# Moving a half tile of the down projection, and new orders in the prologue, in an attention and FFN kernel

## The chip, the cores and the metric

The kernel runs on one core of a Trainium2 chip. The metric is the device time of one execution in microseconds. A core has the engines PE (matmul), DVE (vector), ACT (scalar), POOL (GpSimd) and SP, which here issues all DMAs. Each engine works its own instructions in order; semaphores make it wait for the others.

## The reference, cut to what matters

```python
def reference(x, W_to_kv, W_compress, ..., W1, W2, W3):       # x: (8, 1024, 512)
    x = x + attn(layernorm(x))     # latent = x @ W_to_kv.T; c = latent @ W_compress.T; LN; q, k, v; rope;
                                   # causal softmax over 1024 positions; z = o @ W_comp2lat.T;
                                   # z @ W_to_kv + z @ W_out_res.T + b
    x = x + ffn(layernorm(x))      # W1, W3: (2048, 512), W2: (512, 2048)
    return x

def ffn(x, W1, W2, W3):
    hidden = silu(x @ W1.T) * (x @ W3.T)
    hidden = fwht(hidden)          # Walsh-Hadamard transform over 2048, normalised
    return hidden @ W2.T
```

## The kernel before

There are 8 sequences of 1024 tokens, and each is two blocks of 512 tokens (a = 0 to 15), of four tiles each. Blocks 0 and 1 (sequence 0) get their attention in a prologue. After it stands the main loop: 128 steps k = 16 s + h, one for each sequence s and each of 16 groups h of 128 hidden units. Beside the FFN of sequence s runs the attention of sequence s + 1, cut into slots; slot number and point are tied by slots(s, f), f = 7 h + i.

**A step.** The gate and the up projection of one group are made with seven products instead of eight (a Strassen-Winograd form): of W1, W3 and the tokens x there are seven forms each, in a high and a low fp16 half, and a product is six matmuls of 128x512 (L909 to L911: high by high, high by low, low by high, for two halves of the contraction). The points of a step, i = 0 to 6 in the code, are called 1 to 7 below. In the PSUM banks PF the sums are combined: copy_b (L1299, ACT) copies the first product's bank and product 3 waits for it; copy_p5 (L1305, ACT); sum_c (L1900, DVE) after product 3, for which product 5 waits; sum_e (L1904, DVE) after product 5, for which product 7 waits. silu(k, 0) (L1315, ACT) waits for product 4, silu(k, 1) for product 6. hidden(k, 1) (L1917, DVE) multiplies the second half once silu(k, 1) is there, hidden(k, 0) the first half once product 7 is there; high (L1326, ACT) and low_part (L1925, DVE) split the result into fp16 halves H in the step behind. copy_b of step k + 1 waits for hidden(k, 0), and product 2 of step k + 1 for hidden(k, 1).

**W2's product.** Each four steps fill a quarter of H; down(i) (L960 to L962) multiplies it with W2 (already transformed by Hadamard products), one half of a tile of 128 tokens at a call, six matmuls again. There are four calls in a step, behind points 2, 4, 6 and 7, from step 4 on. out_rows (L1936, DVE) adds a finished tile to the output rows; the two calls of a step stand behind sum_c and behind hidden(k, 1). Attention work of the same point stands behind down().

**The order on DVE and ACT** is written out by hand: fill(k, i) issues the attention work of point i. On DVE a step is: hidden(k - 1, 0), fill 1, low_part, fill 2, sum_c, out_rows, fill 3, (forms_low), fill 4, sum_e, (forms_low), fill 5, hidden(k, 1), out_rows, fill 6, fill 7. On ACT: copy_b, high, fill 1, copy_p5, fill 2, (forms_high), fill 3, silu(k, 0), fill 4, fill 5, silu(k, 1), fill 6, fill 7. Of attention, maxima (L1658 on) and low (L1673) on DVE and exps (L1155, with a load of the exponential's table, and L1160) on ACT lie in these fills, and rope (L1631 on). SP then transposes the probabilities by DMA (PT, L537); pv (L731, PE) waits for them, and outp (L741) for its result in halves.

**Sequence 0** has more beside it: POOL makes the forms of W1 and W3 in WF for h + 2 (L2166 on), ACT and DVE split them into WS (forms_high L1267, forms_low L1876) and SP stores them for the other sequences. W2 is scaled with a power of two that sums() (PE) and scale2() (DVE, v_s2) give, multiplied with blocks of 16 rows of a Hadamard matrix (hadamard2, L861) and split (split2, L1243 ACT, L1864 DVE).

**The prologue** ends with xtrans1 (L833 PE, L1223 ACT): the transposes of the normalised rows of blocks 0 and 1 (xnorm1, L1807 DVE). tokens_high (L1292, ACT) and tokens_low (L1882, DVE) split token parts, tokens_sum (L1892, DVE) makes the others. norms (L1195, ACT) gives the row norms of W1 and W3. Step 0 is made with eight plain block products (first_step, L920 to L922), of which one needs A21, a part of W1 split ahead (a21_high L1256, a21_low L1871). POOL can't go on with the forms of h = 0 before A21 is split. square2 (L1230, ACT) squares W2 with its output thrown into WS, slot 1.

## Time and profile before

| | |
|---|---|
| median of 3 runs | 2115.41 us (2113.53 to 2115.52) |
| the profiled execution | 2113.63 us, of which the span in the trace is 2111.8 us |
| PE busy | 2056.4 us, 97% |
| DVE, ACT, POOL busy | 1409.8 us (67%), 934.1 us (44%), 215.5 us (10%) |
| PE's granted clock, mean | 0.993 |
| products of steps, L909 | 1778 records, 381 ns each |
| W2's product, L960 | 1024 records, 379 ns each |

Matmuls are pipelined: a 128x512 one is on record with 0.38 us, and the next starts some 0.216 us behind it. Times in the trace are from the start of the span.

### The profile page before, as it was taken

To read this page: it belongs to the slowest core of one execution; us is meant where nothing else is said; L and a number is where in the kernel's file an instruction comes from. 1 tells how busy PE (TensorE), PEld (TensorE's weight loads), DVE (VectorE), ACT (ScalarE), POOL (GpSimd) and SP (SyncE) were. 2 spreads that over 40 slices of the span, in tenths; PEclk is the share of its full clock that TensorE was granted. 3 is DMA by queue.
4 is the path that set the end of the run, shared out by engine and by line. 5 is a ranking of instruction groups with operands and counts; after the bars stand their busy time and mean duration, and the time that the engine had idled before them with its cause. 6 is when DMAs were issued, how large, how long until landed. Compare 5 with 4: busy or idle time off the path is not lost. (4 is left out here: it accounts for less than half of the span.)

```text
span 2111.8 us, 26791 instructions
## 1 busy us (share of the span) xinstructions
PE 2056.4 (97%) x9838; PEld 986.4 (47%) x9838; DVE 1409.8 (67%) x2674; ACT 934.1 (44%) x1431; POOL 215.5 (10%) x196
## 2 busy tenths in 40 slices
PE   6789999999999999999999999999999999999999
PEld 3534444444444444444444444444444444444444
DVE  7887888667676676766667676766767666653333
ACT  5857454454434444353543544434444444332221
POOL 2364532101001010011001010010100100000000
PEclk9999999999999999999999999999999999999999
DMA  8544245542463324633346323643146332363211
GB/s 333 208 159 175 106 135 157 167 140 76 119 166 124 128 83 132 159 119 119 111 130 168 117 93 111 153 156 133 61 133 174 124 121 87 113 157 110 90 58 72
DMA packets 231138, 278.62 MB, mean 132 GB/s; under 512 B 178016, under 2 KB 178144, under 8 KB 225632
## 3 DMA queue, kind: packets, MB, share of 16 engines
q1 hardware_dynamic: 231008, 276.91, 42.3%
q8 instruction: 78, 1.28, 0.2%
q14 instruction: 52, 0.43, 0.1%
HBM read 194.81 MB, written 39.85 MB: 111 GB/s over the span
## 5 line engine op out<-in xcount | busy, mean ns | idle before, releaser
L909 PE MATMUL PF<-XF,WS 128*128 128x512 f16 x1778 | 676.7, 381 | 4.0 <-ACT PF L1299 2.9
L910 PE MATMUL PF<-XF,WS 128*128 128x512 f16 x1778 | 675.1, 380 | 0.0
L911 PE MATMUL PF<-XF,WS 128*128 128x512 f16 x1778 | 674.9, 380 | 0.0
L960 PE MATMUL PD<-W2S,H 128*128 128x512 f16 x1024 | 388.1, 379 | 0.0
L961 PE MATMUL PD<-W2S,H 128*128 128x512 f16 x1024 | 388.1, 379 | 0.0
L962 PE MATMUL PD<-W2S,H 128*128 128x512 f16 x1024 | 388.1, 379 | 0.0
L1315 ACT ACTIVATE SH<-PF,afs 128x512 f32<-128x512 f32 x256 | 175.0, 686 | 371.0 <-PE PF L911 369.7
L1925 DVE TENSOR_TENSOR H<-SH,H 128x1024 f16<-128x1024 f32 x128 | 165.6, 1294 | 183.2 <-ACT H L1326 182.8
L909 PEld LDWEIGHTS PF<-XF,WS 128*128 128x128 f16 x1778 | 173.9, 98 | 227.7 <-issue 33.9
L911 PEld LDWEIGHTS PF<-XF,WS 128*128 128x128 f16 x1778 | 174.2, 98 | 210.4 <-issue 1.4
L1917 DVE SCALAR_TENSOR_TENSOR SH<-PF,afs,SH 128x512 f32<-128x512 f32 x256 | 191.6, 749 | 111.8 <-ACT SH L1315 98.8
L910 PEld LDWEIGHTS PF<-XF,WS 128*128 128x128 f16 x1778 | 174.5, 98 | 185.3 <-issue 6.4
L1299 ACT ACTIVATE PF<-PF 128x512 f32<-128x512 f32 x127 | 73.9, 582 | 402.8 <-PE PF L911 284.6
L2146 POOL TENSOR_TENSOR ring<-ring,bb 128x512 f32<-128x512 f32 x56 | 81.9, 1493 | 1156.9 <-DVE V L1614 1156.9
L1936 DVE SCALAR_TENSOR_TENSOR ring<-PD,afs,ring 128x512 f32<-128x512 f32 x224 | 166.4, 743 | 15.6 <-PE PD L962 15.4
L960 PEld LDWEIGHTS PD<-W2S,H 128*128 128x128 f16 x1024 | 100.2, 98 | 120.8
L961 PEld LDWEIGHTS PD<-W2S,H 128*128 128x128 f16 x1024 | 100.2, 98 | 120.8
L962 PEld LDWEIGHTS PD<-W2S,H 128*128 128x128 f16 x1024 | 100.2, 98 | 120.8
L1904 DVE TENSOR_TENSOR PF<-PF,p 128x512 f32<-128x512 f32 x127 | 88.4, 696 | 101.2 <-PE PF L911 100.9
L1326 ACT ACTIVATE H<-SH 128x1024 f16<-128x1024 f32 x128 | 134.2, 1049 | 3.1 <-DVE SH L1917 2.8
L1900 DVE TENSOR_TENSOR PF<-PF,p 128x512 f32<-128x512 f32 x127 | 88.5, 697 | 64.0 <-PE PF L911 63.4
L1315 ACT ACT_TABLE_LOAD x57 | 73.1, 1283 | 11.2 <-DVE H L1925 10.5
(322 smaller groups left out, 2010.2 us busy)
## 6 DMA issues: line engine op xcount, KB each, us to landing
WS<-wscr SPq DMA_DIRECT2D x112, 896.0 KB, 4.9
W2S<-w2scr SPq DMA_DIRECT2D x30, 1024.0 KB, 6.5
ring<-x SPq DMA_DIRECT2D x56, 256.0 KB, 7.0
wscr<-WS SPq DMA_DIRECT2D x16, 896.0 KB, 3.8
out<-ring SPq DMA_DIRECT2D x56, 256.0 KB, 3.1
RAW<-w13t SPq DMA_DIRECT2D x16, 512.0 KB, 3.9
xraw<-xT SPq DMA_DIRECT2D x28, 256.0 KB, 5.7
XF<-w SPq DMA_DIRECT2D x13, 512.0 KB, 18.3
```

The costliest lines, as they stand in the source:

```text
L909: pe.matmul(bank, wh, th, start=i < 2 and j == 0, stop=False, skip_group_check=True)
L910: pe.matmul(bank, wh, tl, start=False, stop=False, skip_group_check=True)
L911: m = pe.matmul(bank, wl, th, start=False, stop=j == 1, skip_group_check=True)
L960: pe.matmul(PD[:, t % 2, :], th, wh, start=j == 0, stop=False)
L961: pe.matmul(PD[:, t % 2, :], th, wl, start=False, stop=False)
L962: m = pe.matmul(PD[:, t % 2, :], tl, wh, start=False, stop=j == 3)
L1315: ac.activation(SH[:, i, :], PF[:, (1 - k % 2, 2)[i], :], ACT.Silu, scale=afs[:, k % NH:k % NH + 1]).then_inc((a_sb, a_sc2)[i], 1)
L1326: ac.activation(H[:, q % 2, k % 4, 0, :], SH[:, :, :].rearrange("p i c -> p (i c)"), ACT.Copy).then_inc(a_hi, 1)
L1900: ve.tensor_tensor(PF[:, 2, :], PF[:, k % 2, :], p5[:, :], ALU.add).then_inc(v_c, 1)
L1917: ve.scalar_tensor_tensor(SH[:, i, :], PF[:, (k % 2, 3)[i], :], afs[:, 16 + h:17 + h], SH[:, i, :], ALU.mult, ALU.mult).then_inc((v_hA, v_ ...
L1925: ve.tensor_tensor(H[:, q % 2, k % 4, 1, :], SH[:, :, :].rearrange("p i c -> p (i c)"), H[:, q % 2, k % 4, 0, :], ALU.subtract).then_inc(v ...
L1936: ve.scalar_tensor_tensor(row, PD[:, t % 2, :], afs[:, 65:66], row, ALU.mult, ALU.add).then_inc(v_ev, 1)
```

## The change

DOWN_AT moves the third half tile of a step from behind product 6 to behind product 5. All else is in the prologue and in steps 0 and 1: A21's parts go to the last two forms of the low half of slot 1 of WS, so they need not wait for square2; first_step's block products come in another order, two of them ahead of xtrans1 of block 1, which now uses four banks; silu(0, 0) waits for the third instead of the second; forms_high(1) comes ahead of block 1's copies, forms_low(1) ahead of tokens_low(7); forms_high(2) goes behind silu(1, 0); the parts of the tokens come in another order; sums() uses bank U, hadamard2(0) no longer waits for v_s2, and scale2 comes one point earlier on DVE.

```diff
+DOWN_AT = (1, 3, 4, 6)
 def xf_no(s, i):
-    return 7 * s + i + 2 if s else (0, 4, 6, 1, 5, 3, 7, 2)[i] + 1
+    return 7 * s + i + 2 if s else (0, 4, 5, 1, 6, 3, 7, 2)[i] + 1
+        a21 = (WS[:, 1, 1, 5, :], WS[:, 1, 1, 6, :])
+        def xbank(a, t):
+            return (X, Y, G, U)[t] if a else (G, U)[t % 2]
...
 # PE: xtrans1
-                b, f = ((G, U), (X, Y))[a][t % 2], xs[t]
+                b, f = xbank(a, t), xs[t]
-                    w.wait_ge(a_xn, n - 2)
+                    w.wait_ge(a_xn, n - 4 if a else n - 2)
 # PE: hadamard2, sums
                 if i < 2:
-                    w.wait_ge(v_s2, 1)
-                    w.wait_ge(a_xn, 4)
+                    w.wait_ge(a_xn, 7 + i)
+                    if i == 1:
+                        w.wait_ge(v_s2, 1)
-                w.wait_ge(a_xn, 3)
-                pe.matmul(G[:, 0:2], ones.broadcast_to([128, 128]), st[:, 2:4], start=True, stop=True).then_inc(p_g2, 1)
+                w.wait_ge(a_xn, 8)
+                pe.matmul(U[:, 0:2], ones.broadcast_to([128, 128]), st[:, 2:4], start=True, stop=True).then_inc(p_g2, 1)
 # PE: first_step
-                    m = block_product((1, 1, 0, 0)[j], j, (0, 3)[j % 2], j % 2 == 0)
+                    m = block_product((1, 0)[j % 2], (0, 2, 1, 3)[j], (0, 3)[j // 2], j < 2)
...
             xtrans1(0, 3)
+            first_step(0)
+            first_step(1)
             w.wait_ge(v_x2, 8)
             xtrans1(1, 0)
...
-                    else:
+                    elif i > 1:
                         first_step(i)
-                    if i in (1, 3, 5, 6):
-                        down(4 * k + (1, 3, 5, 6).index(i) - 1)
+                    if i in DOWN_AT:
+                        down(4 * k + DOWN_AT.index(i) - 1)
 # ACT
             def a21_high():
                 w.wait_ge(g_wm, 2)
-                w.wait_ge(a_sq, 4)
-                ac.activation(WS[:, 1, 0, 6, :], WF[:, 2, :], ACT.Copy).then_inc(a_wh, 1)
+                ac.activation(a21[0], WF[:, 2, :], ACT.Copy).then_inc(a_wh, 1)
             def forms_high(h, part):
-                if h == 1 and part == 1:
-                    w.wait_ge(p_gu, gu_no(0, 4))
+                if h == 1:
+                    w.wait_ge(a_sq, 4)
...
-                w.wait_ge(p_gu, gu_no(k, ((3, 5) if k else (1, 5))[i]))
+                w.wait_ge(p_gu, gu_no(k, ((3, 5) if k else (2, 5))[i]))
             parts_o1(1, 0)
+            a21_high()
             hadamard(9)
             hadamard(10)
-            square2(3)
-            a21_high()
             norms(6, 0)
             norms(6, 1)
+            square2(3)
             forms_high(0, 0)
...
             norms(12, 1)
+            forms_high(1, 0)
+            forms_high(1, 1)
             xtrans1(1, 0)
-            norms(13, 0)
...
                 if k == 1:
-                    norms(14, 1)
+                    tokens_high(0, 4)
+                    norms(13, 1)
...
-                if split:
+                if split and k > 1:
                     forms_high(h + 1, 0)
                     forms_high(h + 1, 1)
...
                 fill(k, 3)
+                if k == 1:
+                    forms_high(2, 0)
+                    forms_high(2, 1)
 # DVE
             parts_o1(1, 0)
-            a21_low()
             norm2(0)
             inverse1(1, 1)
             norm2_root(0)
+            a21_low()
             outp1(1, 0)
+            max1(1, 2)
             forms_low(0, 0)
             forms_low(0, 1)
-            max1(1, 2)
...
             norm2(1)
+            tokens_low(0, 0)
             norm2_root(1)
...
             tokens_low(0, 3)
+            forms_low(1, 0)
             tokens_low(0, 7)
...
-                if s == 0 and f == SUMS_AT + 1:
+                if s == 0 and f == SUMS_AT:
                     scale2()
...
-                if k:
+                if k > 1:
                     hidden(k - 1, 0)
+                if k == 0:
+                    hidden(0, 0)
+                    tokens_low(0, 1)
+                    tokens_sum(0, 2)
                 if k == 1:
+                    tokens_sum(0, 4)
                     tokens_low(0, 2)
+                    tokens_low(0, 4)
                     tokens_sum(0, 6)
```

## Rows read from the trace of the kernel before

**Rows 1.** Busy time by stretch: length, then each engine's busy us, PEclk, DMA share, GB/s.
```profile
100.00:150.00 50.00, 41.07 (x153) 16.88 (x151) 42.34 (x79) 26.86 (x43) 27.94 (x22) 0.90 0.35 129
...
240.00:260.00 20.00, 19.12 (x93) 8.88 (x91) 18.44 (x35) 9.70 (x15) 17.47 (x15) 1.00 0.20 75
...
400.00:800.00 400.00, 398.62 (x1946) 192.33 (x1945) 271.75 (x528) 179.15 (x266) 23.75 (x16) 1.00 0.40 125
```

**Rows 2.** Waits of PE, whole span: us in total, times, longest.
```profile
PE XY L731 <- DMA PT<-Pl: 6.0, 7, 2.5
...
PE PF L909 <- ACT PF L1299: 2.9, 4, 0.9
```

**Rows 3.** Timelines of ACT, DVE and PE, 62 to 82: start, us, operation [idle before].
```profile
66.19 0.42 ACT L1256 ACTIVATE WS<-WX 128x256 f16<-128x256 f32 x1
...
66.63 0.43 DVE L1871 TENSOR_TENSOR WS<-WX,WS 128x256 f16<-128x256 f32 x1 [3.54 <-ACT WS L1256]
...
71.79 0.79 PE L793 MATMUL XY<-Kh,Q 128*128 128x512 f32 x1 [5.29 <-DVE ring L1795]
...
72.86 0.58 ACT L1212 ACTIVATE PT<-PF 128x512 f32<-128x512 f32 x1
...
81.49 0.71 PE L812 MATMUL PF<-PT,H 128*128 128x128 f32 x4 [1.73 <-ACT PT L1212]
```

**Rows 4.** Timelines of PE and DVE, 94 to 141.
```profile
94.08 0.94 PE L833 MATMUL XY<-cst_s,ring 128*128 128x128 f32 x4 [3.22 <-DVE ring L1807]
...
133.27 2.07 PE L861 MATMUL PD<-H,cst_s 128*128 128x512 f32 x2 [5.59 <-DVE afs L1856]
...
140.10 0.75 DVE L1864 SCALAR_TENSOR_TENSOR W2S<-PD,afs,W2S 128x512 f16<-128x512 f32 x1 [0.94 <-ACT W2S L1243]
```

**Rows 5.** Timeline of PE, two waits for transposed probabilities.
```profile
215.24 0.62 PE L731 MATMUL XY<-PT,V 128*128 128x128 f16 x8 [2.52 <-DMA PT<-Pl]
...
703.42 0.51 PE L731 MATMUL XY<-PT,V 128*128 128x128 f16 x6 [0.66 <-DMA PT<-Pl]
```

**Rows 6.** Timelines of PE and ACT, sequence 1, end of step 12.
```profile
568.48 0.38 PE L960 MATMUL PD<-W2S,H 128*128 128x512 f16 x1
...
569.77 0.38 PE L909 MATMUL PF<-XF,WS 128*128 128x512 f16 x1
...
568.68 0.69 ACT L1315 ACTIVATE SH<-PF,afs 128x512 f32<-128x512 f32 x1 [4.51 <-PE PF L911]
...
574.90 0.58 ACT L1299 ACTIVATE PF<-PF 128x512 f32<-128x512 f32 x1 [1.84 <-DVE SH L1917]
...
576.25 0.38 PE L909 MATMUL PF<-XF,WS 128*128 128x512 f16 x1
```

**Rows 7.** Sequence 2, step 13: busy time by stretch, timelines of ACT and PE.
```profile
833.41:839.08 5.67, 5.67 (x28) 2.56 (x27) 5.33 (x21) 0.91 (x1) 0.00 (x0) 1.00 0.50 169
...
839.17 0.58 ACT L1299 ACTIVATE PF<-PF 128x512 f32<-128x512 f32 x1 [4.86 <-PE PF L911]
...
840.25 0.38 PE L909 MATMUL PF<-XF,WS 128*128 128x512 f16 x1
```

**Rows 8.** The same of step 14.
```profile
847.65:853.32 5.67, 5.67 (x28) 2.59 (x27) 5.56 (x6) 0.91 (x1) 0.00 (x0) 1.00 0.47 157
...
853.41 0.58 ACT L1299 ACTIVATE PF<-PF 128x512 f32<-128x512 f32 x1 [4.85 <-PE PF L911]
...
854.50 0.38 PE L909 MATMUL PF<-XF,WS 128*128 128x512 f16 x1
```

**Rows 9.** Timelines of ACT, DVE and PE, sequence 0, steps 13 and 8.
```profile
341.63 0.58 ACT L1299 ACTIVATE PF<-PF 128x512 f32<-128x512 f32 x1 [5.43 <-DVE SH L1917]
...
342.62 0.38 PE L909 MATMUL PF<-XF,WS 128*128 128x512 f16 x1
...
250.98 0.75 DVE L1917 SCALAR_TENSOR_TENSOR SH<-PF,afs,SH 128x512 f32<-128x512 f32 x1
...
258.77 0.39 PE L909 MATMUL PF<-XF,WS 128*128 128x512 f16 x1 [0.88 <-ACT PF L1299]
```

More of the change, by code:

```diff
@@ L119, in xf_no, with t_no @@
 def xf_no(s, i):
-    return 7 * s + i + 2 if s else (0, 4, 6, 1, 5, 3, 7, 2)[i] + 1
+    return 7 * s + i + 2 if s else (0, 4, 5, 1, 6, 3, 7, 2)[i] + 1
+def t_no(s, i):
+    return 4 * s + ({1: 1, 4: 2, 2: 3, 6: 4} if s else {1: 1, 2: 2, 4: 3, 6: 4})[i]
 def wform_no(h, part):
@@ L917, in block_product @@
                 for j in range(2):
-                    wh, wl = (WS[:, f == 2, m, (0, 1, 6, 3)[f], j * 128:(j + 1) * 128] for m in range(2))
+                    wh, wl = (b[:, j * 128:(j + 1) * 128] for b in (a21 if f == 2 else (WS[:, 0, m, f, :] for m in range(2))))
                     th, tl = (XF[:, m, XPART[i], :].rearrange("p (t f c) -> p f t c", t=4, f=2)[:, j] for m in range(2))
@@ L1222, in xtrans1 @@
                 w.wait_ge(p_cp, 8)
-                ac.activation(XS[:, a, :, t * 128:(t + 1) * 128], ((G, U), (X, Y))[a][t % 2].rearrange("p (j c) -> p j c", j=4),
+                ac.activation(XS[:, a, :, t * 128:(t + 1) * 128], xbank(a, t).rearrange("p (j c) -> p j c", j=4),
                               ACT.Copy).then_inc(a_xn, 1)
@@ L1277, in tokens_high @@
                 else:
-                    w.wait_ge(v_t, 4 * s + {1: 1, 4: 2, 2: 3, 6: 4}[i])
+                    w.wait_ge(v_t, t_no(s, i))
                 if s == 0:
@@ L1419, in _ @@
             norms(9, 0)
+            norms(9, 1)
             exps1(1, 3)
@@ L1428, in _ @@
             trans1(1, 3, 1)
-            norms(9, 1)
+            norms(10, 0)
             parts_o1(1, 2)
-            norms(10, 0)
+            norms(10, 1)
             parts_o1(1, 3)
-            norms(10, 1)
             xtrans1(0, 0)
-            norms(11, 0)
             xtrans1(0, 1)
-            norms(11, 1)
             xtrans1(0, 2)
@@ L1441, in _ @@
             tokens_high(0, 3)
+            norms(11, 0)
+            norms(11, 1)
             norms(12, 0)
             norms(12, 1)
+            forms_high(1, 0)
+            forms_high(1, 1)
             xtrans1(1, 0)
-            norms(13, 0)
             xtrans1(1, 1)
-            norms(13, 1)
             xtrans1(1, 2)
@@ L1494, in _ @@
                 if k == 1:
-                    norms(15, 0)
+                    norms(14, 0)
                 fill(k, 0)
@@ L1499, in _ @@
                 if k == 1:
+                    norms(14, 1)
+                    tokens_high(0, 6)
+                    norms(15, 0)
                     norms(15, 1)
-                    tokens_high(0, 6)
                 fill(k, 1)
-                if split:
+                if split and k > 1:
                     forms_high(h + 1, 0)
@@ L1508, in _ @@
                     silu(k, 0)
-                else:
-                    tokens_high(0, 4)
                 fill(k, 3)
+                if k == 1:
+                    forms_high(2, 0)
+                    forms_high(2, 1)
                 fill(k, 4)
@@ L1515, in _ @@
                 if k == 0:
-                    norms(14, 0)
+                    norms(13, 0)
                     tokens_high(0, 2)
@@ L1846, in scale2 @@
                 w.wait_ge(p_g2, 1)
-                k = sv.mark(ve.tensor_copy(st[:, 4:6], G[:, 0:2]))
+                k = sv.mark(ve.tensor_copy(st[:, 4:6], U[:, 0:2]))
                 sv.after(k)
@@ L1870, in a21_low @@
                 w.wait_ge(a_wh, 1)
-                ve.tensor_tensor(WS[:, 1, 1, 6, :], WF[:, 2, :], WS[:, 1, 0, 6, :], ALU.subtract).then_inc(v_wl, 1)
+                ve.tensor_tensor(a21[1], WF[:, 2, :], a21[0], ALU.subtract).then_inc(v_wl, 1)
             def forms_low(h, part):
                 w.wait_ge(a_wh, wform_no(h, part))
+                if h == 1 and part == 1:
+                    w.wait_ge(p_gu, gu_no(0, 4))
                 f = slice(0, 4) if part == 0 else slice(4, 7)
@@ L1886, in tokens_sum @@
                 w.wait_ge(v_xs if s else a_xn, tile_no(2 * s + 1, 3))
-                w.wait_ge(v_t, 4 * s + {1: 0, 4: 1, 2: 2, 6: 3}[i])
+                w.wait_ge(v_t, t_no(s, i) - 1)
                 w.wait_ge(v_xf, xf_no(s, {1: 0, 4: 0 if s else 7, 2: 1, 6: 3}[i]))
@@ L2044, in _ @@
             xnorm1(1, 1)
-            tokens_low(0, 0)
             xnorm1(1, 2)
@@ L2051, in _ @@
             tokens_sum(0, 1)
-            tokens_sum(0, 4)
-            tokens_low(0, 1)
-            forms_low(1, 0)
             forms_low(1, 1)
-            tokens_sum(0, 2)
-            tokens_low(0, 4)
             def fill(k, j):
```

## The prediction

> **What bounds the kernel now.** I read the stages first [rows 1], then who PE waited for in all [rows 2], then the timelines around the long waits [rows 3 to 5]. From 400 to 800 us PE is busy 398.62 of 400 us, and the stages after it look the same: an edit there can win tenths of a microsecond at a place, but it can lose as much as it likes, because nothing is left to absorb a new wait. The start is different: 41.07 of 50 us between 100 and 150. The longest waits are 5.3 us for a DVE eviction [rows 3], 3.2 us for a normalised row and 5.6 us for the scale of W2 [rows 4], and 6.0 us in seven waits for transposed probabilities [rows 2]. So the edits at the start are worth something, up to the point where DVE or ACT is the next late one, and the edit of the steady step must be judged by cover, not by work. PE's work is the same in both kernels; only idle time can change.
>
> **The unit.** A product of a step, or a half tile of W2's product, is six matmuls. The half tile that starts at 568.48 is followed by product 7 at 569.77: 1.29 us [rows 6]. I write the seven products as 1 to 7 and a half tile as H. Before: 1 2 H 3 4 H 5 6 H 7 H. After: 1 2 H 3 4 H 5 H 6 7 H. Product 7 ends when it did, product 6 ends 1.29 us later, and attention work in the fifth place comes 1.29 us later.
>
> **Part 1, the moved half tile: what it covers.** In the fifth place PE waits for a DMA transpose: 2.52 us at 215.24, and 0.66 us at 703.42 [rows 5]; the latter stands for six of one kind, one for each of the sequences 1 to 6, 6.0 - 2.5 = 3.5 us together [rows 2]. H now stands ahead of it. The transposes don't depend on product 6, so the six go (-3.5 us) and the first shrinks by 1.3 us.
>
> **Part 1, what it uncovers.** Product 6 releases ACT's second silu, which releases DVE's second hidden(), behind which stand the eviction of a tile, attention's or the next tokens' DVE work and then the first hidden(). That releases ACT's copy_b, and product 3 of the next step waits for copy_b. Product 3 does not move. So wherever this chain runs without a gap, its cover shrinks by 1.29 us.
> - Step 12 (h = 12) of sequences 1 to 6: silu 568.68, the exponential's table load right behind it, then the high and low halves of the probabilities, hidden(), copy_b at 574.90 for 0.58 us. It ends at 575.48, its semaphore takes 0.06 us, and product 3 starts at 576.25 [rows 6]: cover 0.71 us, new wait 1.29 - 0.71 = 0.58 us.
> - Step 13: DVE is busy 5.33 of the 5.67 us between the second hidden() and the end of the first. What is missing is small gaps between nine dependent 128x4 operations, which can't take up a delay. copy_b 839.17 + 0.58 + 0.06 against product 3 at 840.25: cover 0.44, new wait 0.85 us [rows 7].
> - Step 14: DVE 5.56 of 5.67 us; copy_b 853.41 ends 853.99, product 3 at 854.50: cover 0.45, new wait 0.84 us [rows 8].
> Each wait delays the following products too, and by the next second hidden() DVE is again waiting for PE, so they add up: 2.27 us a sequence, 13.6 us in six. The last sequence has no attention beside it and DVE has room.
> - Sequence 0, where forms are split as well: in step 13 copy_b at 341.63 ends 342.21, product 3 starts at 342.62, cover 0.35: +0.9 us. In step 8 the wait for copy_b is there already, 0.88 us at 258.77, and the second hidden() at 250.98 comes 1.1 us after product 6; it would come at about 252.1: +1.1 us [rows 9]. Before step 4 there is no half tile.
> - The other steps are at no cost: either silu is late for another reason (table load or keys on ACT), or the DVE chain has real gaps (over 2 us in step 4), or the cover is 1.3 us or more. With that cover gone each would cost up to 1.3 us. The second half tile itself needs the low half of H, which is there over 3.5 us before, so its earlier place costs nothing; the eviction of a tile does not wait for it in either kernel, so it gains nothing.
> Sum of part 1: -3.5 - 1.3 + 13.6 + 0.9 + 1.1 = **+10.8 us**.
>
> **Part 2, the start.** *A21's parts:* the low part stood ahead of the root and eviction on DVE and waited 3.54 us for ACT, where the high part at 66.19 stood behind a square of W2 [rows 3]. Now ACT makes it near 63.2, DVE does the roots first and the eviction ends near 67.1, so the scores at 71.79 start some 4.6 us earlier. Next late is ACT, busy throughout: GpSimd's forms come 0.7 us earlier, and the copy at 72.86, for which PE's next transposes wait, starts near 72.2. The square and two norms that were moved leave exps1(1,3) 1.4 us earlier. Behind it the products with P, at 81.49, start 1.3 us earlier, and all up to B11's transposes with them.
> *Two products ahead of B1's transposes:* they fill the 3.22 us wait that ends at 94.08 [rows 4], but they need B11's low part, on DVE behind the second norm: near 91.8. The forms of h = 1 (1.8 us on ACT) now stand ahead of the four copies of B1's transposes, so scale_rows, which waits for the last copy, holds the third product to about 98.7. By this sum step 1 starts 1.7 us earlier. SP is passed by nothing here; its stores and loads of forms follow the same releases.
> *The scale of W2:* sums() uses another bank, the first product with 16-row blocks no longer waits for the scale, and scale2 comes ahead of two bn_stats (1.5 us) on DVE. Against it, forms_high(2) moved behind the latent copy, and forms_low(2), ahead of sums() on DVE, waits for it till near 120.8; the tokens' last parts too are later. The scale comes at about 132.0, and the 5.59 us wait at 133.27 becomes one near 2.3 us before the second such product. PE would be 4 to 5 us ahead there, but then DVE is late: its second split of W2 at 140.10 [rows 4] moves to about 137.9, 2.2 us earlier, and DVE has hardly a gap from there to 160. I take **-2.2 us**. Bounds: all three long waits gone (5.29 + 3.22 + 5.59) would be -14.1 and can't hold with DVE and ACT full; a start in which the new orders lose on ACT what they win on PE is +0.5. For the range I take -5 to +0.5.
>
> **A rule weighed.** Behind the wait at 258.77 [rows 9] the matmuls keep their pitch: the granted clock between 240 and 260 us is 1.00, the 2.4 GHz level [rows 1]. The Trainium skill, *TensorE: Matmul & The Clock Gate*, section *A second HAM failure mode: psum-queue depth-cycling*, says that short idle times of PE between groups of matmuls can make the clock oscillate; by that rule each new wait would be dearer (rival D). The trace speaks against it.
> The page *ScalarE: Activation LUTs*, section *What ACT_TABLE_LOAD costs* in the Trainium skill, adds a drain of about 1.38 us to a switch. Here the exponential follows its 1.28 us load at once. With the drain step 12 would have had no cover at all and a new wait of 1.29 us; the sum would be 4 us higher.
>
> **The sum.** +10.8 - 2.2 = +8.6 us on a span of 2111.8 us and a run of 2113.6 us: 2122.2 us. The median of the runs shown is 1.8 us above the profiled one, so the forecast is **2124 us**, +0.4%.
>
> **Rivals.**
> - A, faster: the chain behind product 6 has more give than I read, in that DVE and ACT catch up before copy_b. The place is steps 12 to 14, the price of each 0.6 to 0.85 us; it decides once less than 0.4 us of the 1.29 us reaches copy_b. Then only the gains stand: -3.5 - 1.3 - 2.2 = -7 us, 2108. For it: out-of-phase gaps exist in other steps. Against: the two windows of DVE, 94 and 98% busy [rows 7, 8]. Chance 0.12.
> - B, no change: the start wins 6 to 8 us, since one of the shifts above isn't eaten by the next engine (the 5.6 us wait and the 1.2 GHz behind it), and part 1 costs what I say: about +4 us, 2119. Chance 0.15.
> - C, the change does less than it says: the half tile covers nothing, as another wait (the copy of ol to the output product, 0.1 us of cover left) takes the place of the six: +3.5 more, 2127.5. Chance 0.05.
> - D, the clock: PE drops to 1.2 GHz at each of some 20 new waits, as it did at the 5.59 us one, behind which the matmul pair took 2.07 us [rows 4]. A product of 1.29 us at half the clock costs 1.3 us more: +26 us, 2150. Against it, the short waits of before left the clock alone [rows 1, 9]. The page named above is its source. Chance 0.01.
> My forecast has 0.67. Its own range is 2119 to 2129. For 8 in 10 the range must reach into B and a little further: 2115 to 2130. 0.2% (4.2 us) is about what a measurement of this kernel can tell from no change. Faster by over 0.2%: 0.11; within: 0.19; slower: 0.70.
>
> **What would show it.** In the profile after: no wait of PE for PT in the fifth place of sequences 1 to 6, and one near 1.2 us in sequence 0; 18 new waits of product 3 for ACT's copy_b in steps 13 to 15 (one after each of steps 12 to 14), 0.6 to 0.85 us each, so that PE's wait for that line grows from 2.9 us to some 18 us; PE busy 2 us less of each 248 us of a sequence; the first product of step 1 near 108.5 and W2's second split near 138. I am wrong if that line's wait stays below 8 us, or if the steps reach 400 us over 4 us ahead.

## The result

| | before | after |
|---|---|---|
| median | 2114.56 us (2113.53 to 2115.52) | 2126.73 us (2126.21 to 2128.30) |
| span in the trace | 2111.8 us | 2125.1 us |
| PE busy | 2056.4 us | 2063.1 us |
| DVE, ACT, POOL busy | 1409.8, 934.1, 215.5 us | 1397.2, 932.0, 213.4 us |
| PE's granted clock, mean | 0.993 | 0.992 |

Both medians are of runs on the same chip. The ratio is 1.0060, interval 1.0050 to 1.0071: the changed kernel is slower by 12.2 us. The forecast was 2124.0 us with a range of 2115 to 2130; the time is 2.7 us above it, inside.

**Who PE waited for**, whole span of the changed kernel: us in total, times, longest.

```profile
PE PF L925 <- ACT PF L1316: 15.5, 23, 2.2
...
PE PF L818 <- ACT PT L1231: 4.6, 1, 4.6
...
PE PF L936 <- DVE XF L1906: 3.1, 1, 3.1
PE PD L877 <- DVE W2S L1885: 3.0, 5, 1.1
PE XY L746 <- DMA PT<-Pl: 2.6, 3, 1.0
```

L925 is the product (L909 before), L1316 is copy_b (L1299). Against [rows 2] this wait went from 2.9 us in four to 15.5 us in 23, and the one for the transposed probabilities from 6.0 us in seven to 2.6 us in three.

**Busy time by stretch** of the changed kernel: length, then PE, PEld, DVE, ACT, POOL, PEclk, DMA share, GB/s.

```profile
400.00:800.00 400.00, 398.06 (x1941) 191.41 (x1938) 269.24 (x535) 178.38 (x265) 23.64 (x16) 1.00 0.40 125
...
100.00:150.00 50.00, 43.16 (x160) 17.32 (x159) 44.20 (x81) 28.78 (x48) 28.13 (x24) 0.93 0.36 126
```

Beside [rows 1], the start has PE 2.1 us busier between 100 and 150, and the steady stretch 0.56 us less busy in 400 us. That stretch holds three of the new waits and two of the covered ones, and busy time shows each wait too short (below). The forecast's sign "PE busy 2 us less" in each sequence did not come: on record PE is idle 1.86 us of a sequence against 0.65 us, 1.2 us more, because the covered wait goes out of the same sum and each new wait is shown short.

**Where the new waits are**, timeline of PE after: start, us, operation [idle before].

```profile
577.20 0.39 PE L925 MATMUL PF<-XF,WS 128*128 128x512 f16 x1 [0.42 <-ACT PF L1316]
...
593.68 0.39 PE L925 MATMUL PF<-XF,WS 128*128 128x512 f16 x1 [0.68 <-ACT PF L1316]
...
608.78 0.39 PE L925 MATMUL PF<-XF,WS 128*128 128x512 f16 x1 [0.68 <-ACT PF L1316]
```

These three stand in each of the sequences 1 to 6, with the same three lengths; the last three are at 1829.28, 1845.74 and 1860.84. The bracket is 0.17 us short of what is lost, because an idle time begins at the modelled end of a matmul (0.38 us) and not at the pitch (0.216 us): the real waits are 0.59, 0.85 and 0.85 us.

**The shift between the two traces** shows it without brackets: I took the start of the same half tile and of the same product 3 in both traces. Where their difference (after minus before) grows, time is lost. At product 3 behind the first of the waits, for example, it is 577.20 - 576.25 [rows 6] = +0.95 us, and at the half tile in front of it 575.32 - 574.95 = +0.37 us: 0.58 us in between. Over the eighteen places the shift grows by 0.56 to 0.60 us behind step 12 and by 0.84 to 0.87 us behind steps 13 and 14.

| place | forecast | after against before |
|---|---|---|
| start, up to step 4 | -2.2 | -1.6 |
| sequence 0, PT wait of step 6 | -1.3 | -1.5 |
| sequence 0, behind step 8: wait for copy_b | +1.1 | +1.35 |
| right behind it: 1.2 GHz for 3 us | 0 | +0.8 |
| sequence 0, step 12: a new PT wait | 0 | +0.9 |
| sequence 0, behind steps 13 and 14 | +0.9 | +0.5 |
| sequences 1 to 6, behind steps 12, 13, 14 | +13.6 | 6 x 2.28 = +13.7 |
| sequences 1 to 6, PT wait of step 5 | -3.5 | -3.5 (five of -0.77, one of +0.3) |
| sequences 1 to 6, output product in step 4 | 0 | 6 x 0.23 = +1.4 |
| the rest, pieces of 0.1 to 0.2 (among them 0.09 behind step 15 of each of six sequences) | 0 | +1.2 |
| sum | +8.6 | +13.3 |

### The profile page after: what moved, and what is told of

Its sections match the earlier page's. It is cut to its first block and busy times, and to the rows that moved or that the text cites. A ratio compares the mean times of both kernels' runs of the same rounds, so it can differ in the third digit from the quotient of the medians.

```text
span 2125.1 us, 26793 instructions
## 1 busy us (share of the span) xinstructions
PE 2063.1 (97%) x9838; PEld 983.1 (46%) x9838; DVE 1397.2 (66%) x2674; ACT 932.0 (44%) x1431; POOL 213.4 (10%) x196
## 3 DMA queue, kind: packets, MB, share of 16 engines
q8 instruction: 78, 1.28, 0.2%
## 5 line engine op out<-in xcount | busy, mean ns | idle before, releaser
L925 PE MATMUL PF<-XF,WS 128*128 128x512 f16 x1778 | 677.1, 381 | 18.3 <-ACT PF L1316 15.5
L1941 DVE SCALAR_TENSOR_TENSOR SH<-PF,afs,SH 128x512 f32<-128x512 f32 x256 | 191.4, 747 | 188.6 <-ACT SH L1332 187.8
L925 PEld LDWEIGHTS PF<-XF,WS 128*128 128x128 f16 x1778 | 173.9, 98 | 250.7 <-issue 32.1
L1949 DVE TENSOR_TENSOR H<-SH,H 128x1024 f16<-128x1024 f32 x128 | 161.1, 1259 | 159.0 <-ACT H L1343 158.7
L1316 ACT ACTIVATE PF<-PF 128x512 f32<-128x512 f32 x127 | 73.9, 582 | 360.5 <-DVE SH L1941 187.6
L1960 DVE SCALAR_TENSOR_TENSOR ring<-PD,afs,ring 128x512 f32<-128x512 f32 x224 | 166.2, 742 | 14.9 <-PE PD L979 14.7
```

Source lines behind the costliest of these rows:

```text
L925: pe.matmul(bank, wh, th, start=i < 2 and j == 0, stop=False, skip_group_check=True)
L1941: ve.scalar_tensor_tensor(SH[:, i, :], PF[:, (k % 2, 3)[i], :], afs[:, 16 + h:17 + h], SH[:, i, :], ALU.mult, ALU.mult).then_inc((v_hA, v_ ...
L1949: ve.tensor_tensor(H[:, q % 2, k % 4, 1, :], SH[:, :, :].rearrange("p i c -> p (i c)"), H[:, q % 2, k % 4, 0, :], ALU.subtract).then_inc(v ...
L1960: ve.scalar_tensor_tensor(row, PD[:, t % 2, :], afs[:, 65:66], row, ALU.mult, ALU.add).then_inc(v_ev, 1)
```

## The experiments

Each kernel ran 5 to 11 times in turn with the kernel before. The times are medians, each ratio is to the kernel before in the same series (its medians are 2114.1 to 2115.0 us), and a difference to another kernel is between medians of two series unless both ran in one. "Shift" is that of the table above, against the trace of before if nothing else is said.

### The half tile alone, and the start alone

The kernel before with only

```diff
-                    if i in (1, 3, 5, 6):
-                        down(4 * k + (1, 3, 5, 6).index(i) - 1)
+                    if i in (1, 3, 4, 6):
+                        down(4 * k + (1, 3, 4, 6).index(i) - 1)
```

> The kernel before with the third half tile behind product 5 in every step, and nothing of the prologue changed. Theory (the steps alone cost): the six PT waits of sequences 1 to 6 go, 18 new waits for copy_b of 0.59, 0.85 and 0.85 us come, and the wait for the copy of ol 0.2 us in each sequence; all that the changed kernel shows from the start of sequence 1 on (+12.6 us) stays, and the differences of sequence 0 come too, so the time is 12 to 15 us above the kernel before, 2127 to 2130. Rival (the start's edits carry a part of the loss, by what they queue on ACT and DVE): 5 to 10 us above, under 2125.

Measured: 2130.26 us, ratio 1.0072 (1.0058 to 1.0086): +15.3 us, just above the 2127 to 2130 of the expectation. From step 4 to the last sequence the shift grows by 15.1 us, with the pieces of the table but for the clock, and with 0.2 to 0.3 us more in three places (step 12 of sequence 0, step 14 of sequence 3, step 5 of sequence 4).

The changed kernel with

```diff
-DOWN_AT = (1, 3, 4, 6)
+DOWN_AT = (1, 3, 5, 6)
```

> The changed kernel with the third half tile back behind product 6, so only the edits of the prologue and of steps 0 and 1 are left. Theory: they gain 1.6 us at step 4, as in the changed kernel, and nothing takes it back: 1 to 2.5 us below the kernel before, 2112 to 2113.6. Rival (the lower clock behind step 8 and the PT wait at 314 us in sequence 0 belong to the new start and not to the half tile): equal to the kernel before or up to 1 us above.

Measured: 2113.37 us, ratio 0.9992 (0.9983 to 1.0001): 1.6 us less, which the interval doesn't tell from nothing. In its trace neither the wait of 0.76 us at 314 us nor the lower clock behind step 8 is there, so neither comes from the start's edits alone. The PT wait stands in both kernels with the early half tile; the lower clock stands in the changed kernel and not in the one with the half tile alone (more below). The whole loss, 13.4 us from this kernel to the changed one, is the half tile's. The trace of this kernel is of the fastest of its 11 runs (2110.31 us): it is 2.9 us ahead of before at step 4, where the changed kernel, with the same code up to there, is 1.6 us ahead.

### Only in steps 12 to 14

The kernel before with the early place in 18 of its 128 steps:

```diff
+def down_at(k):
+    s, h = divmod(k, NH)
+    return (1, 3, 4, 6) if 0 < s < 7 and h in (12, 13, 14) else (1, 3, 5, 6)
...
-                    if i in (1, 3, 5, 6):
-                        down(4 * k + (1, 3, 5, 6).index(i) - 1)
+                    if i in down_at(k):
+                        down(4 * k + down_at(k).index(i) - 1)
```

> The kernel before with the half tile behind product 5 only in steps 12, 13 and 14 of sequences 1 to 6, 18 steps of 128. Theory: 0.59 + 0.85 + 0.85 = 2.3 us in each sequence, 13.7 us in all: 2128.3 (2127 to 2129.5), more than the whole change costs. Rival (the waits only stand where PE, run late by something else, would have stood too, so most of the cost is in other steps): below 2121.

Measured: 2129.92 us, ratio 1.0072 (1.0059 to 1.0084), +15.0 us, just above the expected 2127 to 2129.5. The shift grows by 0.59, 0.85 and 0.85 us and another 0.09 us in each of the six sequences, 14.3 us in sum. The rest does not come from these steps: the trace is 1.9 us behind that of before at step 4 already, with the same instructions up to there, which is the clock of the start (below). These 18 steps cost as much as the early place in all steps (+15.3 us): what it wins and loses in the others cancels out.

### Only where it covers something

The changed kernel with the same function, and the condition

```diff
-    return (1, 3, 4, 6) if 0 < s < 7 and h in (12, 13, 14) else (1, 3, 5, 6)
+    return (1, 3, 4, 6) if k == 6 or s and h == 5 else (1, 3, 5, 6)
```

> The changed kernel with the half tile behind product 5 only in step 6 of sequence 0 and in step 5 of the later sequences, where it covers the wait for PT, and behind product 6 in all others. Theory: the gains stand without the losses: -1.6 (start), -1.5 (step 6), -0.75 in each of six sequences = -4.5, in sum -7.6 us, 2107 (2105 to 2109). If the wait for the copy of ol in step 4 had a part in covering the PT wait, 0.2 us less in each. Rival (PE's saved time is given back at the next wait of each sequence, since copy_b or the transposes then come too late): 2110 to 2113.

Measured: 2106.82 us, ratio 0.9962 (0.9949 to 0.9974), as expected: 8.1 us below the kernel before. It beats both kernels. The shift falls by 1.3 us at step 6 and by 0.75 to 0.84 us at step 5 of five sequences; in sequence 4 it rises by 0.14 us. PE's waits, whole span:

```profile
PE PF L929 <- ACT PF L1320: 3.1, 5, 0.9
...
PE XY L750 <- DMA PT<-Pl: 1.9, 2, 1.2
```

L929 and L1320 are the product and copy_b, L750 is pv. The two waits left are those of step 6 and of sequence 4. Nothing came in the place of the other five: the saved time is not given back later in the sequence.

### A shorter chain instead of a later half tile

The changed kernel; DVE's order in the same 18 steps:

```diff
                     hidden(k - 1, 0)
+                    if late:
+                        out_rows((k - 1) // 4 - 1, 2 * ((k - 1) % 4))
...
                 hidden(k, 1)
-                out_rows(k // 4 - 1, 2 * (k % 4))
+                late = 0 < s < 7 and h in (12, 13, 14)
+                if not late:
+                    out_rows(k // 4 - 1, 2 * (k % 4))
                 fill(k, 5)
```

> The changed kernel; in steps 12, 13 and 14 of sequences 1 to 6 DVE evicts the finished tile (0.67 us) behind the first hidden() instead of between the second and the first. The work is the same, only the chain from product 6 to the next copy_b is 0.67 us shorter where DVE sets it. Theory (cover of that chain): the waits after steps 13 and 14 fall from 0.85 to about 0.2 us each, the one after step 12 stays at 0.59, since there ACT's table load and the exponentials set the chain: 6 x 1.3 = 8 us less than the changed kernel, 2118.8 (2117 to 2121). Rival (PE waits for something else that only ends with copy_b, or DVE loses the time elsewhere): within 2 us of the changed kernel, 2125 to 2127.

Measured: 2119.02 us, ratio to the kernel before 1.0021 (1.0012 to 1.0029), 7.7 us below the changed kernel. Against the trace of the changed kernel the shift is -0.66 us behind each step 13 and each step 14, twelve times, and 0.00 behind each step 12. PE's waits for copy_b fell from 23 to 11, and what is left in sequence 1 is one:

```profile
PE PF L925 <- ACT PF L1316: 7.4, 11, 2.2
...
576.93 0.39 PE L925 MATMUL PF<-XF,WS 128*128 128x512 f16 x1 [0.43 <-ACT PF L1316]
```

The waits behind steps 13 and 14 are so short now (0.85 - 0.66 = 0.19 us) that they have no bracket. DVE after that edit, step 13 of sequence 1:

```profile
590.14 1.22 DVE L1906 TENSOR_TENSOR Pl<-XS,Ph 128x1024 f16<-128x1024 f32 x1
591.27 0.75 DVE L1941 SCALAR_TENSOR_TENSOR SH<-PF,afs,SH 128x512 f32<-128x512 f32 x1
591.94 0.74 DVE L1960 SCALAR_TENSOR_TENSOR ring<-PD,afs,ring 128x512 f32<-128x512 f32 x1
```

L1941 is hidden(), L1960 out_rows, now behind it; its pitch of 0.66 us is what each of the twelve waits lost. This is the test of the mechanism: the half tile is where it was, and only the place of out_rows changed. Behind step 12 nothing changed, as expected: there the table load and the exponentials stand on ACT ahead of copy_b.

### Step 8 of sequence 0, and the clock

The changed kernel with the late place in this one step (down_at with the condition k != 8):

> The changed kernel with the half tile back behind product 6 in step 8 of sequence 0 alone. Theory: the wait of product 3 for copy_b after that step falls from 2.2 to 0.9 us (-1.35), and the drop of the clock to 1.2 GHz right behind it (0.8 us) belongs to it and goes too: 2.1 us less at 273 us, 2124.6. Rival (the clock drops there for what PE did before, whatever this wait): only 1.35 us less, and the matmuls behind the wait still at 0.63 us instead of 0.38.

Measured: 2124.52 us, ratio to before 1.0048 (1.0035 to 1.0060), 2.2 us below the changed kernel. The shift against it is -1.34 us at product 3 behind step 8 and a further -0.81 us at the next step. PE in the changed kernel:

```profile
257.11 0.39 PE L925 MATMUL PF<-XF,WS 128*128 128x512 f16 x1 [2.23 <-ACT PF L1316]
257.34 0.44 PE L926 MATMUL PF<-XF,WS 128*128 128x512 f16 x1
257.57 0.63 PE L927 MATMUL PF<-XF,WS 128*128 128x512 f16 x1
258.00 0.63 PE L925 MATMUL PF<-XF,WS 128*128 128x512 f16 x1
```

Its busy time in the next 2 us (the clock is the number before the last two):

```profile
258.00:260.00 2.00, 2.00 (x6) 1.03 (x5) 1.58 (x2) 1.95 (x5) 0.00 (x0) 0.50 0.00 0
```

The same place in the kernel with the late half tile in step 8, and in the one with the half tile alone:

```profile
255.19 0.39 PE L929 MATMUL PF<-XF,WS 128*128 128x512 f16 x1 [0.89 <-ACT PF L1320]
255.41 0.38 PE L930 MATMUL PF<-XF,WS 128*128 128x512 f16 x1
```

```profile
260.23 0.39 PE L909 MATMUL PF<-XF,WS 128*128 128x512 f16 x1 [2.23 <-ACT PF L1299]
260.45 0.38 PE L910 MATMUL PF<-XF,WS 128*128 128x512 f16 x1
```

A pitch of 0.43 us and 0.63 us on record go with a granted clock of 0.50, the 1.2 GHz level. With a wait of 0.89 us it stays at 2.4 GHz. With a wait of 2.2 us it fell in the changed kernel and in the one with the eviction behind hidden() (2.24 us at 256.53), and not in the one with the half tile alone, so the length of the wait alone doesn't decide it. The 18 shorter waits of each run with the early half tile left the clock at 1.00.

### The start, piece by piece

A21's parts alone (kernel before, new place in memory and order). With the place a wait moves too: that for product 5 of step 0 goes from forms_high(1) on ACT to forms_low(1) on DVE.

```diff
+        a21 = (WS[:, 1, 1, 5, :], WS[:, 1, 1, 6, :])
...
 # ACT
-                if h == 1 and part == 1:
-
-                    w.wait_ge(p_gu, gu_no(0, 4))
+                if h == 1:
+                    w.wait_ge(a_sq, 4)
...
+            a21_high()
             hadamard(9)
             hadamard(10)
-            square2(3)
-            a21_high()
             norms(6, 0)
             norms(6, 1)
+            square2(3)
...
 # DVE
+                if h == 1 and part == 1:
+                    w.wait_ge(p_gu, gu_no(0, 4))
...
-            a21_low()
             norm2(0)
             inverse1(1, 1)
             norm2_root(0)
+            a21_low()
```

> The kernel before with A21's parts in their new place in memory and order on ACT and DVE, nothing else. Theory: the wait of 5.3 us for the eviction falls below 1 us, the transposes behind it keep their wait for ACT (4.5 us), the products with P start 1.3 to 1.8 us earlier, and step 1 about as much; from the scale of W2 on DVE takes a part back: 0 to 1.5 us below the kernel before. Rival (ACT, full in that stretch, gives the gain back before the transposes of the tokens): step 1 at the same time as before, no change.

Measured: 2111.84 us, ratio 0.9988 (0.9979 to 0.9996). The scores start at 67.22 against 71.79 us, and the products with P at 79.26 against 81.49. The gain of 2.6 us is more than the 0 to 1.5 us expected, and it came another way: step 1 starts at 110.13 against 110.17 us, as the rival said, since PE ran at a granted clock of 0.51 from 94 to 100 us (0.72 before). The trace is 1.7 us ahead at sums() and 2.7 us at step 4; between 130 and 140 us, behind the wait for W2's scale, its granted clock is 0.83 against 0.66.

The scale of W2 alone (kernel before):

```diff
                 if i < 2:
-                    w.wait_ge(v_s2, 1)
                     w.wait_ge(a_xn, 4)
+                    if i == 1:
+                        w.wait_ge(v_s2, 1)
...
-                w.wait_ge(a_xn, 3)
+                w.wait_ge(a_xn, 4)
-                pe.matmul(G[:, 0:2], ...)
+                pe.matmul(U[:, 0:2], ...)
...
-                if s == 0 and f == SUMS_AT + 1:
+                if s == 0 and f == SUMS_AT:
                     scale2()
```

> The kernel before with the scale of W2 alone as in the changed kernel: sums in bank U, the first product with 16-row blocks without a wait for the scale, scale2 one point earlier on DVE. Theory: the 5.6 us wait for the scale near 133 us shrinks by the two bn_stats (1.5 us) and one product, to about 3.5 us, but the splits behind it are DVE's, so 0.3 to 1.5 us are left at step 4: 2113.5 to 2114.7. Rival (all three start edits depend on one another and this one alone gives nothing): within 0.3 us of before at step 4.

Measured: 2111.07 us, ratio 0.9985 (0.9976 to 0.9994); 3.4 us below before, more than the 0.3 to 1.5 us expected. Its trace is 0.7 us behind before at sums() and 2.3 us ahead at step 4.

Both together, without the third edit (the order of the first products, of the token parts and of the forms of h = 1, and the banks):

> The kernel before with the two start edits that gained alone (A21's parts: -2.6 us by the medians, the scale of W2: -3.4), without the third, the new order of the first products, of the token parts and of the forms of h = 1. Theory (the third edit gives back what the two win, since E2, with all three, gained 1.6 us): 2110 to 2112, at or below the better of the two alone, and 2 us or more below E2. Rival (both edits gain the same microseconds, those before DVE is late, and the third costs nothing): 2112 to 2114.

Measured: 2109.11 us, ratio 0.9972 (0.9961 to 0.9982), 5.6 us below before and a little below the expected 2110 to 2112. The two about add up (2.6 and 3.4 us alone), and the third edit costs: the kernel with all three is at 2113.37, ratio 0.9992 (0.9983 to 1.0001). By the traces it starts step 1 at 108.20 us, 2.0 us ahead of this one (110.20), and is 2.3 us behind it at step 4.

From the first product of step 1 to that of step 3, in the kernel before, then with the two edits, then with all three:

```profile
110.17:153.26 43.09, 34.16 (x122) 14.23 (x122) 35.40 (x76) 19.50 (x33) 25.46 (x22) 0.88 0.40 146
```

```profile
110.20:147.20 37.00, 31.87 (x121) 13.42 (x121) 34.13 (x74) 19.19 (x33) 22.25 (x21) 0.95 0.42 155
```

```profile
108.20:149.53 41.33, 33.65 (x122) 13.72 (x122) 36.35 (x75) 22.05 (x39) 22.90 (x21) 0.92 0.38 139
```

The work of PE is the same but for an instruction or two, so what differs is idle time (8.9, 5.1 and 7.7 us) and the clock (0.88, 0.95 and 0.92). Of the 4.3 us between the last two, 2.5 us are waits; for the other 1.8 us PE is busy longer, at the lower clock: behind the wait for the latent copy PE has 0.63 and 0.51 from 118 to 122 us with all three edits, and 1.00 from 118 to 124 us with two. So a part of what the two edits win, and of what the third loses, is clock that follows the waits. What sets the level behind a wait was not tried here.

The same with the half tile in the chosen steps:

> The same with the half tile behind product 5 in step 6 of sequence 0 and step 5 of the later ones, as in the run with chosen steps. Theory: about 6 us below the kernel without it (as 2106.8 stands to 2113.4), 2104 to 2106, and the fastest of all. Rival (the third edit of the start is needed to hold the gain): 2107 or more.

Measured: 2102.96 us, ratio 0.9943 (0.9930 to 0.9957), 11.8 us below the kernel before and below the expected 2104 to 2106: the fastest kernel of the study.

Which part of the third edit costs it? DVE in step 1, in the run with the start alone and then in the fastest kernel:

```profile
120.79 1.23 DVE L1900 TENSOR_TENSOR WS<-WX,WS 128x1024 f16<-128x1024 f32 x1 [3.49 <-ACT WS L1284]
```

```profile
118.47 1.23 DVE L1883 TENSOR_TENSOR WS<-WX,WS 128x1024 f16<-128x1024 f32 x1 [1.90 <-ACT WS L1272]
```

DVE stands longer for the high halves of h = 2 ahead of the scales and sums. So I put them back (kernel with chosen steps and all start edits):

```diff
-                if split and k > 1:
+                if split and k:
                     forms_high(h + 1, 0)
                     forms_high(h + 1, 1)
...
-                if k == 1:
-                    forms_high(2, 0)
-                    forms_high(2, 1)
```

> The run with chosen steps and all start edits, with one thing put back: in step 1 ACT makes the high halves of the forms of h = 2 ahead of silu(1, 0) and of the latent copy, as in the kernel before. In that run and the changed kernel DVE stood 3.5 us for them, ahead of the scales and sums; with the old order it stood 1.1 us. Theory (this one move is what the third start edit loses): DVE reaches the scales some 2.5 us earlier, W2's scale and splits come 2 us earlier, step 4 as well: 2104 to 2105.5, against 2106.8. If the latent copy, now 1.8 us later, is what PE then waits for, half of it is lost: 2105.5 to 2106. Rival (the loss lies in the order of the token parts or of the banks): no change, 2106.5 to 2107.5.

Measured: 2106.50 us, ratio 0.9966 (0.9952 to 0.9979), no change against 2106.82. DVE's wait fell to 1.28 us (from 3.27 in the run with chosen steps, 3.49 with the start alone), but PE's for the latent copy (L1132, ACT; L695 are the transposes behind it) grew from 2.24 us in both those runs to 3.92. Here, and then in the fastest kernel:

```profile
121.26 0.69 PE L695 MATMUL XY<-cst_s,PB 64*128 64x64 f32 x4 [3.92 <-ACT PB L1132]
```

```profile
120.28 0.46 PE L682 MATMUL XY<-cst_s,PB 64*128 64x64 f32 x4 [2.41 <-ACT PB L1116]
```

Then two norms behind that copy, too (the pair norms(15, 0) and norms(15, 1) from step 1's second point to behind its fourth):

> The run before this one (forms of h = 2 ahead) with two of W3's last norms (1.2 us on ACT) put behind the latent copy of step 1. In that run PE stood 3.9 us at 121.3 us for this copy, and in the run with two start edits only 2.1 to 2.4: ACT has 3 us of norms and token parts in step 1 that the third start edit moved there. Theory (ACT's queue ahead of the latent copy is what that edit costs): the wait falls to about 2.7 us, sums() and W2's scale come 1.2 us earlier, 2105.3 (2104.3 to 2106). Rival (the scales on DVE, which need these norms, set the sums then): no change at step 4, 2106 to 2107.

Measured: 2106.97 us, ratio 0.9964 (0.9950 to 0.9977). PE's wait fell as the theory says, but DVE then stands for the norms, as the rival says:

```profile
120.81 0.48 PE L695 MATMUL XY<-cst_s,PB 64*128 64x64 f32 x4 [2.69 <-ACT PB L1132]
...
122.96 0.18 DVE L1571 TENSOR_SCALAR st<-st 128x24 f32<-128x24 f32 x1 [2.73 <-ACT ring L1218]
```

Each of the two moves only changes who is late. What is shown is that the first two start edits win 5.6 us and that the third takes a good part of it back between step 1 and step 4; that the ACT work it puts into step 1 (norms and token parts that stood ahead of step 0) is the reason fits both runs, but no run that takes all of it out and leaves the rest of the edit was made, so this stays open. The clock is no simple answer either: with the two norms moved it has its best mean between steps 1 and 3 of the kernels with the third edit (0.96, against 0.92), and PE is idle 8.5 us, against 7.7 in the run before it.

## Why the prediction came out as it did

**Cover in steps 12 to 14: right.** The forecast read 0.58, 0.85 and 0.84 us from the end of copy_b to product 3 [rows 6 to 8]; the traces give 0.59, 0.85, 0.85 (the bracket and 0.17 us), six times over. The 15.5 us on record for this line, with 0.17 us more for each of the 18, are the "some 18 us" that were forecast. That DVE's small gaps can't take up a delay held as well. The other page that was weighed, *ScalarE: Activation LUTs* of the Trainium skill, section *What ACT_TABLE_LOAD costs*, adds a drain of about 1.38 us to a switch of tables and would have given the wait behind step 12 its full 1.29 us. The 0.59 us measured speak against it here, and for the row in which the exponential follows its table load at once. ACT after, end of step 12:

```profile
576.57 0.58 ACT L1316 ACTIVATE PF<-PF 128x512 f32<-128x512 f32 x1 [1.84 <-DVE SH L1941]
```

It has the same 1.84 us ahead of it as in [rows 6], and comes 1.67 us later by the clock of the trace: 1.29 us of the half tile and 0.37 us that PE was late anyway.

**The six PT waits: right, with one exception.** Five went. In sequence 4 one stands, longer than the 0.66 us of before [rows 5], beside that of step 6 and an extra one in step 12 of sequence 0:

```profile
213.52 0.62 PE L746 MATMUL XY<-PT,V 128*128 128x128 f16 x8 [0.98 <-DMA PT<-Pl]
...
1208.33 0.51 PE L746 MATMUL XY<-PT,V 128*128 128x128 f16 x6 [0.87 <-DMA PT<-Pl]
...
314.38 0.95 PE L746 MATMUL XY<-PT,V 128*128 128x128 f16 x14 [0.76 <-DMA PT<-Pl]
```

The first was forecast at 1.2 us. The last is a step that the forecast didn't take: in step 12 of sequence 0 the probabilities' exponential stands on ACT behind silu(k, 1), so the transposes of the probabilities come later too. silu(k, 1) starts at 303.19 against 302.76 us though PE was 0.9 us ahead of before at that point; the first transpose is issued at 307.39 against 306.96; and the product with V, in the sixth place, has no half tile more ahead of it than before. "The other steps are at no cost" looked at copy_b alone, not at the attention work that stands behind the same silu.

**Rival C's mechanism is there, without its consequence.** In step 4 of each sequence the copy of ol, behind hidden(), ends 1.29 us later. ACT and PE after, then before:

```profile
445.01 0.31 ACT L1183 ACTIVATE ol<-oh 64x128 fp32r<-64x128 f32 x1 [1.68 <-DVE oh L1704]
...
445.42 0.47 PE L756 MATMUL XY<-Mh,oh 128*128 128x512 f32 x1
```

```profile
442.83 0.31 ACT L1164 ACTIVATE ol<-oh 64x128 fp32r<-64x128 f32 x1 [1.67 <-DVE oh L1683]
...
444.19 0.58 PE L741 MATMUL XY<-Mh,oh 128*128 128x512 f32 x1
```

Before, the copy ended 444.19 - 443.14 = 1.05 us ahead of PE; 1.29 - 1.05 = 0.24 us is the new wait, and the shift says 0.23. It is too short for a bracket. The forecast named this wait only as one that could replace the six; it comes on top of them, at 1.4 us in six. So the term "the other steps are at no cost" failed here too: the gaps of DVE in step 4 were read, the chain to the output product was not priced.

**Sequence 0.** Behind step 8 the +1.1 us was +1.35, and 1.36 in the run with the half tile alone: the 0.2 us of give that I had read into the chain weren't there. The clock drop right behind it was rival D's mechanism, in one place; the forecast had nothing for it. The page *TensorE: Matmul & The Clock Gate* of the Trainium skill, section *A second HAM failure mode: psum-queue depth-cycling*, says that short idle times of PE between groups of matmuls make the clock oscillate. For waits under a microsecond the trace speaks against it, as forecast: 18 of them left the granted clock at 1.00. The term for step 13 (+0.9) was too large: the shift is +0.18 us behind step 13, and +0.34 us behind step 14, for which there was no term. The PT wait just ahead, in step 12, gives DVE time to catch up, which fits but wasn't tried.

**Part 2: near in sum, not right in its parts, and in part luck.** -1.6 us against -2.2; five profiled runs with this start (after, the start alone, the chosen steps, the eviction behind hidden(), the late half tile in step 8) have -1.6, -2.9, -1.6, -2.5 and -2.2 us at step 4. PE after, the waits that the forecast spoke of:

```profile
66.55 0.50 PE L808 MATMUL XY<-Kh,Q 128*128 128x512 f32 x1 [0.42 <-DVE ring L1816]
...
72.30 0.69 PE L818 MATMUL PF<-cst_s,PB 128*128 128x128 f32 x2 [4.56 <-ACT PT L1231]
...
91.89 0.59 PE L936 MATMUL PF<-XF,WS 128*128 128x512 f16 x1 [3.12 <-DVE XF L1906]
...
99.88 0.27 PE L886 MATMUL XY<-WX,cst_s 128*128 128x256 bf16 x1 [0.94 <-ACT XS L1242]
...
133.17 1.13 PE L877 MATMUL PD<-H,cst_s 128*128 128x512 f32 x2 [0.55 <-DVE afs L1877]
```

The 5.29 us wait [rows 3] became 0.42 us, and ACT was next late: the copy that ends the next wait starts at 71.67 us (forecast 72.2, before 72.86), and the products with P start at 79.67, 1.8 us earlier (forecast 1.3). The two products start at 91.89 (91.8), but then run at the 1.2 GHz level (2.5 to 2.6 us for a block of six, 1.29 before), which the forecast left out: scale_rows comes at 99.88 instead of 98.7, step 1 at 109.7 instead of 108.5, and W2's scale frees PE at 133.17, while the forecast had DVE's scale at 132.0. What failed here is the term for the first products, by 1.2 us. DVE's second split of W2 starts at 138.75 (137.9), 1.35 us earlier than before instead of 2.2. That the start could win 5.6 us if the third edit were left out was not seen. Rival B had a number of this size (6 to 8) and named the 5.6 us wait and the 1.2 GHz behind it; the runs with fewer edits win at that place, and the changed kernel doesn't.

**The sum.** +8.6 us was forecast on the profiled run, +13.3 was there; by the medians 12.2 us. The 4.7 us are the output product (1.4), the PT wait of step 12 (0.9), the clock (0.8), the start (0.6) and pieces of 0.1 to 0.2 us. The first two are places where the 1.29 us reach another waiting instruction than copy_b; the small pieces were not followed up. That the total came out inside the range rests on the large term of steps 12 to 14 being right; the four pieces that were put at nothing all cost time.

## What to carry to other kernels

A unit of work that is moved on a full engine is paid by whatever hangs on the work that it is put in front of: follow every chain from there to the next instruction that waits on the full engine, and compare each cover with the length of the unit. Here that gave eighteen waits as 0.58, 0.85 and 0.84 us, measured as 0.59, 0.85 and 0.85; the chains that were not followed (to the output product, and to the transposes of step 12) cost another 2.3 us. A choice of place needn't be the same in all steps: put the unit early only in the steps where it covers a wait (-6.6 us), not in all (+13.4 us). Where a long wait goes at a start with several full engines, judge each edit by itself, since two of three won and the third took some of it back, and read the clock behind each wait beside the waits.

## What the runs showed of the hardware

**A transpose that lands late beside an instruction fetch.** In sequence 4 the DMA transposes of step 5 were late with the early half tile. DMA queues and issues of the changed kernel, the stretch of sequence 3 (954 to 962 us) and then that of sequence 4 (1202 to 1211 us). The last number of an issue's line is us from issue to landing:

```profile
q1 hardware_dynamic: 1408, 1.25, 53.4%
...
PT<-Pl SPq DMA_TRANSPOSE x1, 2.4
```

```profile
q1 hardware_dynamic: 1305, 1.08, 42.7%
q8 instruction: 1, 0.02, 0.8%
...
PT<-Pl SPq DMA_TRANSPOSE x1, 4.0
```

```profile
1204.32 1.25 SPq L552 DMA_TRANSPOSE PT<-Pl  x1
1205.61 2.01 SPq L478 DMA_DIRECT2D xraw<-xT  x2
```

The second transpose took 4.0 us to land instead of 2.4, and the next two issues on SP took 2.01 us together instead of 1.05. The other runs with the early half tile have the same: 3.8 us with the chosen steps, with either start, and 4.2 us with the half tile alone. One transfer of the instruction queue (16 KB, there are 78 in the run) lies in that stretch and none in that of sequence 3. In the kernel before and in the one with the start alone there is such a transfer in the stretch of sequence 4 as well, but the transposes landed in 2.4 us and the transfers of x that follow were the late ones (RAW 5.5 and 4.9 us, against 4.1 in sequence 3 of the kernel before). That the fetch delays whatever is under way beside it fits all six traces; it was not tried by itself.

**The start's clock differs from run to run.** With the same instructions up to there, PE at 82 to 86 us had a granted clock of 1.00 in the profiled run of before, and 0.62 and 0.53 in that of the half tile alone. By step 4 this run is 1.5 us behind. The run with the early place in steps 12 to 14 only has 0.65 and 0.50 there and is 1.9 us behind.

```profile
82.00:84.00 2.00, 2.00 (x14) 2.00 (x13) 1.55 (x8) 1.68 (x6) 0.00 (x0) 0.62 0.77 326
84.00:86.00 2.00, 2.00 (x10) 1.70 (x10) 0.12 (x1) 0.58 (x2) 0.00 (x0) 0.53 0.41 147
```

A difference of 1 to 2 us at the start is therefore read from medians, or between two points of one trace, and not from the spans of two profiles.
